# The first layer norm's sums of tile i+2 are issued ahead of the FFN's up projection instead of behind it

## The reference

```python
def _layernorm(x, axis=-1, eps=1e-5):
    m = jnp.mean(x, axis=axis, keepdims=True)
    v = jnp.var(x, axis=axis, keepdims=True)
    return (x - m) / jnp.sqrt(v + eps)
# _L0_attn_ref, on the layer norm of x
delta = sigmoid(x @ W_t.T + b_t) * 0.99 + 0.01
h = scan of h[s] = exp(A * delta[s]) * h[s-1] + (x @ W_b.T + b_b)[s]
y = (h @ W_c.T + b_c + x * D) @ W_o.T + b_o
# _L0_ffn_ref, on the layer norm of the sum
h = bitlinear(x, w_fc) + gate * (x @ v.T @ fast_b.T @ u.T)
r = maximum(h, 0)
out = bitlinear(r * r, w_proj)
```

## Time and profile before

| what | value |
|---|---|
| median of 2 runs | 2111.58 us (2083.09 and 2140.06) |
| the profiled execution | 2082.17 us, of which 2080.6 us are the span from the first to the last instruction of the slowest core |
| spans of the 8 cores | 2066.9 to 2080.6 us |
| mean granted TensorE clock of the cores | 0.818 to 0.832 of full speed |
| TensorE busy with matmuls | 66% of the span |
| VectorE busy | 43% |
| ScalarE busy | 16% |

### The profile page before, as it was taken

How to read it: one execution, slowest core, us unless ns; L and a number is a source line. 1 busy time by engine, 2 the same in 40 slices (tenths; PEclk the granted TensorE clock), 3 DMA queues, 4 the chain that set the end, 5 groups by cost and what they waited for, 6 DMA issues and landing times.

```text
span 2080.6 us, 14729 instructions; the slowest of 8 cores (2066.9 to 2080.6 us)
## 1 busy us (share of the span) xinstructions
PE 1382.1 (66%) x5667; PEld 621.4 (30%) x5768; DVE 896.3 (43%) x925; ACT 332.6 (16%) x392; POOL 27.0 (1%) x42
## 2 busy tenths in 40 slices
PE   1544355324288849884987589758966895798498
PEld 0211155301033314331432134223422342343143
DVE  1777778745623271237124621552164316413410
ACT  1111122110131013102300220022003200310220
POOL 0000000000000000000000000000000000000000
PEclk9766677657699979996998699779977997899799
DMA  6233355341021513241324123412431151225033
GB/s 126 101 121 110 112 162 168 125 151 41 0 103 71 191 41 122 74 169 40 122 85 182 36 101 110 173 41 81 160 123 61 61 189 54 80 102 182 26 117 141
DMA packets 73236, 221.43 MB, mean 106 GB/s; under 512 B 4512, under 2 KB 37280, under 8 KB 54720
## 3 DMA queue, kind: packets, MB, share of 16 engines
q1 hardware_dynamic: 60208, 167.79, 23.9%
q0 software_dynamic: 12960, 52.69, 7.1%
HBM read 189.28 MB, written 33.55 MB: 107 GB/s over the span
## 4 chain that ended last, share of the span: by engine, by line
PE 58%; DVE 26%; issue 6%; ACT 4%; DMA 4%; DVEq 0%; POOL 0%; POOLq 0%; ACTq 0%; SPq 0%
PE pb L893 21%; PE pb L948 21%; PE pb L766 6%; PE pb L356 3%; PE pb L441 2%; DVE tls L862 2%; DVE tls L621 2%; DVE xnb L631 2%; DVE xnb L872 2%; DVE cb L382 2%; DVE xnb L551 2%; DVE cb L383 2%; DMA woT_b<-woT 2%; DMA wsl<-wprojT 1%; PE pb L559 1%
## 5 line engine op out<-in xcount | busy, mean ns | idle before, releaser
L893 PE MATMUL pb<-xnb,wcmb_st 128*128 128x512 bf16 x2003 | 475.0, 399 | 138.7 <-DVE but L657 85.4
L948 PE MATMUL pb<-r2b,wproj_st 128*128 128x512 bf16 x2008 | 441.7, 379 | 2.8 <-DMA wproj_st<-wproj_sc 0.5
L893 PEld LDWEIGHTS pb<-xnb,wcmb_st 128*128 128x128 bf16 x2048 | 207.5, 102 | 406.2 <-issue 188.3
L948 PEld LDWEIGHTS pb<-r2b,wproj_st 128*128 128x128 bf16 x2048 | 200.1, 98 | 243.1 <-issue 2.5
L923 DVE TENSOR_TENSOR r2b<-r2b 128x4096 bf16<-128x4096 bf16 x32 | 73.4, 2292 | 390.7 <-ACT r2b L914 390.7
L966 DVE TENSOR_TENSOR xn<-xn,pb 128x512 f32<-128x512 f32 x64 | 44.0, 688 | 366.2 <-PE pb L948 366.2
L914 ACT ACTIVATE r2b<-pb 128x512 bf16<-128x512 f32 x256 | 152.1, 597 | 292.1 <-PE pb L893 291.9
L766 PE MATMUL pb<-yb,woT_b 128*128 128x512 bf16 x503 | 127.7, 418 | 13.0 <-DVE yb L747 12.5
L839 ACT ACT_TABLE_LOAD x8 | 10.3, 1283 | 718.4 <-DVE statB L833 718.4
L559 PE MATMUL pb<-xb,ones_b 128*128 128x512 bf16 x63 | 28.2, 627 | 125.6 <-DVE xb L552 125.6
L303 PE MATMUL pb<-GTb,v_b 16*128 16x512 bf16 x64 | 22.1, 450 | 115.3 <-DVE wr L310 115.2
(11 more groups left out here) (106 smaller groups left out, 1143.6 us busy)
## 6 DMA issues: line engine op xcount, KB each, us to landing
wcmb_st<-wcmb_sc SPq DMA_DIRECT2D x64, 1024.0 KB, 4.8
wproj_st<-wproj_sc SPq DMA_DIRECT2D x64, 1024.0 KB, 4.9
x_s<-xT POOLq DMA_DIRECT2D x8, 2048.0 KB, 8.6
yT<-xn POOLq DMA_DIRECT2D x8, 2048.0 KB, 9.2
wsl<-wfcT SPq DMA_DIRECT2D x4, 2048.0 KB, 10.1
wslB<-wfcT SPq DMA_DIRECT2D x4, 2048.0 KB, 9.8
wcmb_sc<-wr POOLq DMA_DIRECT2D x8, 1024.0 KB, 4.1
wsl<-wprojT SPq DMA_DIRECT2D x4, 2048.0 KB, 10.0
```

The source lines that it names most:

```text
L893: i2 = te.matmul(pb[b][:], wcmb_st[:, hs % 2, dc, (hc % 4) * 128:(hc % 4 + 1) * 128], xnb[:, p, dc], start=(dc == 0), stop=(dc == DCH - 1))
L948: i2 = te.matmul(pb[b][:], wproj_st[:, oc % 2, kc, :], r2b[:, kc], start=(kc == 0), stop=(kc == hch - 1))
```

## The change

Three edits belong together. In the main loop `emit_front1(i + 2)` is called ahead of `emit_ffnA(i)` instead of behind it, for the six tiles i = 0 to 5 that have a tile i+2. The squares go into `yb` instead of `xnb` (in all eight calls), since the up projection of tile i reads that half of `xnb` afterwards. And VectorE waits for the second layer norm's sums of tile i (`stats2`), the last reader of `yb`, instead of the last matmul of the up projection.

```diff
-           "tls": 0, "nz": 0}
+           "tls": 0, "nz": 0, "stats2": 0}
...
             if j >= 2:
-                wait(ve, "vector", "s_T", ffa_last[j - 2])
+                wait(ve, "vector", "s_T", run["stats2"])
             wait(ve, "vector", x_sem(j), xin_count(j))
-            ve.tensor_tensor(out=xnb[:, p], in0=src, in1=src, op=ALU.mult)
+            ve.tensor_tensor(out=yb[:], in0=src, in1=src, op=ALU.mult)
...
-                i2 = te.matmul(pb[1][:], ones_b[:], xnb[:, p, dc],
+                i2 = te.matmul(pb[1][:], ones_b[:], yb[:, dc],
...
-        st = ctr["s_T"]
+        st = run["stats2"] = ctr["s_T"]
...
     for i in range(nt):
+        rs1 = emit_front1(i + 2) if i + 2 < nt else None
         emit_ffnA(i)
-        rs1 = emit_front1(i + 2) if i + 2 < nt else None
         emit_ffnB(i)
```

## The result

| | before | after |
|---|---|---|
| median | 2082.89 us (10 runs) | 2114.51 us (11 runs) |
| lowest | 2081.25 us | 2110.12 us |
| profiled execution, span | 2080.6 us | 2109.4 us |
| ratio after to before | | 1.0145, 95% interval 1.0114 to 1.0177 |

The forecast was 2119 us, in a range from 2106 to 2148. (In this and the later comparisons a few executions were disturbed and much longer; the medians contain them and the ratios leave them out, so where the two differ the ratio is the one to go by.) The change makes the kernel slower, though by less than 2%.

What follows compares the result with a forecast made beforehand. TensorE and VectorE take turns, so the path changing between them bounds the kernel. 135.2 us come, 96.1 go, 6 x 0.35 go for the clock: +37.0 on 2082.17 us, 2119 us; range 2106 to 2148.

Steps and rivals of the forecast that it cites:

- The cover: Down projection's start: the last squared piece takes 2.29 us, needed only after 24 matmuls, about 5.2 us; no stop.
- The size: Whole kernel: 135.2 us come, 96.1 go, six times 0.35 saved by shorter sums; +37.0 us.
- the clock's part of the sum: Layer-norm sums 0.35 us shorter in each of six tiles, no difference from chunk 2; ends +29 and +46 us overall.
- the bound of 0.75: First layer norm's sums at the low clock: at most 0.75 us less than tile 3's, at the other end 0.5 more.
- The bounds of the sum: Both clock effects at their ends in all six tiles: 1.65 us less or 1.2 more each; 2111 to 2128 us.
- The bound of 0.7 us more for the stretch behind chunk 2: Rest of the up projection: 0.9 us less to 0.7 more than now; no difference taken.
- rival 1: TensorE's new stops leave sums and up projection at the low clock for the whole upper bound; +46 us, 2128 us; chance 0.24.
- "Only the gap counts" (2): VectorE readies square and copy before L655, so sums fill TensorE's wait; 96 us go, at best nothing comes; chance 0.03.
- my best case for it, 1986 us: Whole kernel if the 96 us between the projections go and nothing comes on the path.
- "No table loads between neighbours" (3): ScalarE's loads ahead of the Ln and Exp L604 leave the path; 15.4 us less, 2104 us; chance 0.03.
- The gap closed (4): Rival that it doesn't: down projection waits for the last squared piece in six tiles; 18 us more, 2137 us; chance 0.03.
- The clock stayed at 1.00 in the unbroken stretch (5): Rival that the clock falls in long dense projections; price at most +659 us, 2778 us; chance 0.01.

Runs made afterwards that it cites:

- experiment 4's repetition: Changed kernel plus matmuls with unread results in TensorE's two stops: 138 (82 for tile 0) ahead of the sums, 24 ahead of chunk 2; 2090.95 us.
- experiment 3: Changed kernel, but only square and copy stay ahead of the up projection; the sums and their chain go behind it again; 2005.85 us, ratio 0.9605 to before.
- experiment 5: Changed kernel, but square and copy moved ahead of L655 and the chain after the sums behind the up projection; 2007.40 us, ratio 0.9650 to before.
- experiment 1: Changed kernel with emit_front1(i + 2) back behind emit_ffnA(i), so only the buffer and its wait differ from before; ratio 1.000 to before.
- experiment 2: Changed kernel with the chain after the sums (ScalarE's Ln and Exp) behind the up projection; timed again: 2067.2 us, ratio 0.9930 to before.

## Why the prediction was right, and where it was too high

**The mechanism** held at each place that was named. L551 starts 11.81 us behind L655 (forecast 11.80). The sums start 18.57 behind it (18.56). ScalarE gets to the first ReLU through the Exp L604, and chunk 2 stops for about 6 us. The idle time ahead of L559 is 237.9 us (roughly 240). From L655 to L948 tile 3 takes 87.67 us (about 89). The cover held too: the down projection waits for no squared piece, and `x_s` and `yb` were free.

**The size** was 37 us and came out at 28.8 in the spans and 31.6 in the medians; the difference between the spans is the one to be compared with the sum. The step that was mis-sized is the clock's part of the sum. I took the sums as 0.35 us shorter than tile 3's and no difference behind the second stop. Measured the same way, from the first of the sums to L893, the six tiles took 5.22, 5.98, 4.82, 6.03, 5.72 and 4.82 us, 5.43 in the mean, against 6.29 in tile 3 before: 0.86 less, even a little beyond the bound of 0.75. From chunk 2 the mean was 53.9 against 54.34, 0.4 less. Together that is 0.9 us a tile, 5 of the 8 us. Another 3 lie in the start of the tiles, 2.0 us earlier, and in the rest of the loop. The median of 2114.51 lies only 4.5 us from the forecast, closer than the sum earned: it is 3.5 us above the profiled execution. The reason for the bias is to be seen in the rows: before, tile after tile lost nearly the same time at the low clock, at the long end (6.2 to 6.3 us for the sums in tiles 1 to 5); after, the losses scatter. I took one side of a scatter for its middle. The two losses of a tile do not scatter apart from each other: in tiles 0, 2 and 5 the sums were short (4.82 to 5.22 us) and the rest from chunk 2 long (54.40 to 54.61), in tiles 1, 3 and 4 it was the other way round (5.72 to 6.03, and 53.18 to 53.50). The bounds of the sum add the two ends as if they could fall together; why they do not is not shown. The bound of 0.7 us more for the stretch behind chunk 2 follows from no row either; the longest of the six was 0.3 above tile 6's.

**The rivals.** The low clock did not last longer (rival 1): it lasted shorter. What it costs is shown by experiment 4's repetition, 23.6 us in all. "Only the gap counts" (2) fails for the change, by the order of VectorE's stream as argued, and experiments 3 and 5 show what is needed to make it come true. They also show that my best case for it, 1986 us, was not so far off: 2006. "No table loads between neighbours" (3) fell: L690, L591, L604 and L914 each have their own load of 1.28 us in the new order as well. What the Trainium skill says in "ScalarE: Activation LUTs" ("Table sets: the hidden batching unit") would spare some of them; the trace of this program differs, before and after. The gap closed (4). The clock stayed at 1.00 in the unbroken stretch (5), so the current limit of which the Trainium skill tells in "TensorE: Matmul & The Clock Gate", Part 1, did not show here.

**Not tried:** a kernel without the table loads; they stand on no line of the kernel's own code, so what they cost is not shown. Why the clock is kept behind one short stop and lost behind another was not tried either.

## What to carry to other kernels

When a stage is moved to close a gap, price every engine's share of it by itself: here VectorE's share was worth moving, TensorE's and ScalarE's were not, and a cut between them turned +1.5% into -4% (experiment 3). An engine keeps its order, so a moved wait delays all that stands behind it; move the producer early and leave the waiting instructions where their input has long been ready. A short stop of TensorE can cost more than its length: in these runs a stop of 4 to 7 us made the up projection behind it another 1.4 to 2.9 us longer than the 51.8 us at the full clock.

## What the runs showed of the hardware that was not expected

- The clock behind a stop of TensorE ahead of chunk 2: kept at 1.00 behind 3.21 us in one tile of experiment 5, lost behind 3.37 us in the next (0.76 in the 3 us around the restart). The length of the stop does not decide alone: in the same run the up projection took 51.80 us behind a stop of 3.31 us, as at the full clock, and 53.18 us behind one of 2.58. Behind 0.2 to 1.8 us, there and ahead of other groups, the clock was kept, and behind 4.08 and more it was lost, in all tiles that were looked at.
- In 17 tiles of six traces (the kernel before, the changed one and experiments 1 to 3) the stop ahead of chunk 2 lay between 4.08 and 4.54 us, and the recorded stretch behind it between 54.59 and 54.13: the two add up to 58.67 or 58.68 us every time. Within these bounds a shorter stop gave nothing back. Why is not shown.
- With the same instructions and the same kind of stop ahead, sixteen matmuls that begin at the low clock took from 4.82 to 6.03 us, and 3.45 us at the full clock throughout.
- ScalarE's table load for the ReLUs does not run ahead of the wait in its block. In experiment 2 ScalarE was free from 1176.65 on, but loaded only when chunk 0 had come:

```profile
1176.02 0.63 ACT L695 ACTIVATE e1t<-e1t 16x512 f32<-16x512 f32 x1
1192.96 1.28 ACT L919 ACT_TABLE_LOAD   x1 [16.32 <-PE pb L898]
```

That would explain the last 0.39 us of stop ahead of chunk 2, since the load takes 1.28; no run leaves it out.
